# Transformer layer on one core: routing arithmetic spread over three feed-forward units, the first unit's high terms first, one transposed row of maxima earlier

## The reference, cut to what matters

```
xn = _layernorm(x)
a  = sliding_window_attn(xn)                     # 16 heads of 16, window of 64 to each side
h  = layer_norm(a + xn, g1, b1)
f  = gelu(h @ W1 + c1) @ W2 + c2                 # 256 -> 1024 -> 256
attn_out = layer_norm(f + h, g2, b2)
scores = einsum('bsh,eh->bse', xn, gate_w)       # 8 experts, each token goes to one
chosen = argmax(scores)
ffn_out = xn + (xn @ expert_w[chosen].T)         # written as einsum with a one-hot
out = x + attn_out + ffn_out
```

## Time and profile before

| | before |
|---|---|
| median of 3 runs (lowest, highest) | 1375.54 us (1372.25, 1376.72) |
| profiled execution: time, span | 1372.64 us, 1370.9 us |
| mean granted clock of TensorE | 0.968 |
| busy: PE, DVE, ACT, POOL | 1160.1, 899.2, 737.7, 672.8 us |
| share of the chain that ended last: PE, ACT, DVE, issue, POOL, DMA | 55%, 12%, 9%, 7%, 4%, 4% |
| HBM traffic | 122 GB/s over the span |

### The profile page before, as it was taken

How to read it: one execution, slowest core, us unless ns; L and a number is a source line. 1 busy time by engine, 2 the same in 40 slices (tenths; PEclk the granted TensorE clock), 3 DMA queues, 4 the chain that set the end, 5 groups by cost and what they waited for, 6 DMA issues and landing times.

```text
span 1370.9 us, 32155 instructions
## 1 busy us (share of the span) xinstructions
PE 1160.1 (85%) x11726; PEld 704.4 (51%) x11726; DVE 899.2 (66%) x2097; ACT 737.7 (54%) x1498; POOL 672.8 (49%) x864
## 2 busy tenths in 40 slices
PE   0636898899979898798979999899988999799987
PEld 0323446574637546384546646374464746365356
DVE  8563657675677766676577756676576756676355
ACT  1322675448553575537654485627754375645761
POOL 6311565427751465517653375605655277524861
PEclk9956999999999999999999999999999999999999
DMA  8494279234952359234863249433692349513010
GB/s 268 122 214 151 92 142 206 67 109 121 222 140 87 131 110 212 74 117 118 188 166 99 88 118 218 115 109 110 146 198 68 112 122 221 141 54 103 7 28 32
DMA packets 126230, 176.43 MB, mean 129 GB/s; under 512 B 11104, under 2 KB 95968, under 8 KB 122976
## 3 DMA queue, kind: packets, MB, share of 16 engines
q1 hardware_dynamic: 103168, 132.43, 33.4%
q0 software_dynamic: 22912, 41.95, 16.5%
HBM read 82.85 MB, written 85.07 MB: 122 GB/s over the span
## 4 chain that ended last, share of the span: by engine, by line
PE 55%; ACT 12%; DVE 9%; issue 7%; POOL 4%; DMA 4%; another core or an unknown queue 2%; SPq 0%; POOLq 0%; DVEq 0%; ACTq 0%
PE bank L1264 7%; PE bank L1358 7%; PE bank L1164 5%; PE bank L1167 5%; PE bank L1165 5%; ACT pool L1046 5%; PE bank L1438 3%; PE bank L1257 3%; PE bank L1434 3%; PE bank L1435 3%; DVE m_sb L757 2%; PE bank L1232 2%; ACT bank L1101 2%; PE bank L1196 2%
## 5 line engine op out<-in xcount | busy, mean ns | idle before, releaser
L1046 ACT ACTIVATE pool<-bank 128x512 f32<-128x512 f32 x512 | 287.9, 599 | 114.5 <-PE bank L1264 111.6
L757 DVE TENSOR_REDUCE m_sb<-bank 128x2 f32<-128x384 f32 x512 | 260.7, 552 | 98.4 <-PE bank L1272 84.3
L494 POOL TENSOR_SCALAR_AFFINE_SELECT pool<-pool 128x512 f32<-128x512 f32 x256 | 181.7, 710 | 161.8 <-ACT pool L1046 122.4
L432 POOL TENSOR_TENSOR rs<-ve,neghalf 128x1 f32<-128x1 f32 x64 | 36.8, 575 | 324.5 <-DVE ve L834 272.3
L1264 PE MATMUL bank<-q_s,k_s 128*128 128x256 f16 x1024 | 180.6, 276 | 11.1 <-ACT pool L1046 5.3
L1358 PE MATMUL bank<-pool,v_a 128*32 128x256 f32 (+2 forms) x2560 | 159.1, 339 | 11.9 <-POOL pool L499 8.2
L1257 PE MATMUL bank<-k_s,q_s 48*64 48x192 f16 x2048 | 95.5, 262 | 68.9 <-DVE m_sb L757 49.2
L1032 ACT ACTIVATE xn<-bank 128x256 f32<-128x256 f32 x120 | 46.1, 384 | 191.0 <-PE bank L1167 180.9
L1264 PEld LDWEIGHTS bank<-q_s,k_s 128*128 128x128 f16 x1024 | 74.7, 97 | 133.9 <-issue 103.7
L849 DVE TENSOR_TENSOR pool<-bank,pool 128x512 f16<-128x512 f32 x128 | 88.2, 689 | 73.1 <-ACT pool L1060 60.9
L499 POOL TENSOR_SCALAR_AFFINE_SELECT pool<-pool 128x512 f32<-128x512 f32 x208 | 135.3, 650 | 0.0
(11 more groups left out here) (168 smaller groups left out, 2433.2 us busy)
## 6 DMA issues: line engine op xcount, KB each, us to landing
pair_dram<-pool SPq DMA_DIRECT2D x96, 256.0 KB
xn<-xs_dram SPq DMA_DIRECT2D x40, 384.0 KB, 3.7
ys_dram<-xn SPq DMA_DIRECT2D x120, 128.0 KB, 1.8
q_s<-pair_dram SPq DMA_DIRECT2D x32, 384.0 KB
k_s<-pair_dram SPq DMA_DIRECT2D x32, 384.0 KB
x_sb<-in_L_attn_x SPq DMA_DIRECT2D x8, 1024.0 KB, 6.5
res_dram<-in_L_attn_x SPq DMA_DIRECT2D x8, 1024.0 KB, 7.0
res_dram<-xn POOLq DMA_DIRECT2D x8, 1024.0 KB, 8.0
```

What stands on the lines that cost most here:

```text
L494: nc.gpsimd.affine_select(out=p, in_=p, compare_op=ALU.is_ge, fill=0.0, base=0, pattern=[[0, 4], [1, 2 * W]], channel_multiplier=-1).then_ ...
L757: nc.vector.tensor_reduce(m_sb[:, 4 * g + par:4 * g + 4:2, t], max_bank(j, par)[:, 0:2 * WIN].rearrange("p (h c) -> p h c", h=2), AX.X, AL ...
L1046: nc.scalar.activation(prob[:, (k + 2) % 3, par::2, :], TB[par][:, :].rearrange("p (h q) -> p h q", h=2), ACT.Exp, scale=EXP_SCALE).then_i ...
```

## The change

Three things are moved; no arithmetic is added or left out.

1. On DVE, the three pieces of routing no longer stand together ahead of `gelu_low(1)`: tiles come behind `gelu_low(1)`, positions behind `gelu_low(2)`, experts behind `gelu_low(3)`.
2. On PE, unit 0 of W1 waits for the high half alone, runs its four matmuls on `tr_h`, then waits for `tr_l` and runs the other two. (With it, the first projection unit of the next batch waits for three instead of four low halves.)
3. On PE and DVE, `max_cols` of group 2 goes to the head of step 10's new work: ahead of `scores(b, 27)` and of `maxima(b, 27)`.

```diff
@@ vector, d_stage
                         for i in range(2, 4):
                             n1_low(b, i)
-                        if not last:
-                            routing_tiles(b + 1)
-                            routing_positions(b + 1)
                     if u == 1 and not last:
+                        routing_tiles(b + 1)
+                    if u == 2 and not last:
+                        routing_positions(b + 1)
+                    if u == 3 and not last:
                         routing_experts(b + 1)
@@ vector, turn
+                    if k in MAX_AT:
+                        max_cols(b, MAX_AT[k])
                     if 1 <= k and k - 1 + LEAD < STEPS:
                         maxima(b, k - 1 + LEAD)
-                    if k in MAX_AT:
-                        max_cols(b, MAX_AT[k])
@@ tensor, qk_third
-                        pe.wait_ge(xT_l.sem, xT_l.at(b, 4))
+                        pe.wait_ge(xT_l.sem, xT_l.at(b, 3 + u))
@@ tensor, w1_unit
-                pe.wait_ge(nT_l.sem, nT_l.at(b, DC * hf + DC))
                 if u == 0:
+                    pe.wait_ge(nT_h.sem, nT_h.at(b, DC))
                     pe.wait_ge(r1.sem, r1.at(b, T))
+                else:
+                    pe.wait_ge(nT_l.sem, nT_l.at(b, DC * hf + DC))
...
+                if u == 0:
+                    for c in range(DC):
+                        nc.tensor.matmul(UB[0][:, :], w1_h[:, c, fs], tr_h[:, c, s], start=c == 0, stop=False)
+                    for c in range(DC):
+                        nc.tensor.matmul(UB[0][:, :], w1_l[:, c, fs], tr_h[:, c, s], start=False, stop=False)
+                    pe.wait_ge(nT_l.sem, nT_l.at(b, DC))
+                    for c in range(DC):
+                        mm = nc.tensor.matmul(UB[0][:, :], w1_h[:, c, fs], tr_l[:, c, s], start=False, stop=c == DC - 1)
+                    mm.then_inc(u_ps.sem, 1)
+                    return
```

## The result

| | before | after |
|---|---|---|
| median (lowest, highest) | 1374.11 us (1372.25, 1376.72) | 1352.49 us (1350.63, 1353.46) |
| profiled execution: time, span | 1372.64, 1370.9 us | 1350.63, 1348.9 us |
| mean granted clock | 0.968 | 0.968 |

To find where, I cut both traces at marks that every batch has: the start of DVE's one-hot, and PE's four transposes of maxima (groups 0 to 3, `max_cols`).

The account below looks back on a forecast made before the run. The chain is mostly PE, with routing stages set by when POOL's send ends. Terms -5.2 (routing stages) and -2 (step 10) sum to -7.2 on 1372.64, giving 1365.4; median forecast 1368.5 us, range 1354 to 1381.

Parts of the forecast that it names:

- The low-half wait of the projection: Next batch's first projection unit on PE: the wait is hidden behind step 18, gain 0, bounds -0.5 and 0.
- The feed-forward stage: Seven routing stages: unit 8 held instead of unit 7, net 0.75 us earlier each, -5.2 in all.
- a lump for the clock: Routing stage, PE: half clock after its longer stand costs up to 1.7 us, taken as 0.75 per stage.
- The new wait: PE in the routing stage: about 2.4 us for `maxima(2)` ahead of `scores(3)`, none ahead of unit 4.
- Which result is held: Routing stage: `scores(4)` and unit 7 escape the hold; unit 8 and `scores(5)` are held.
- the bound of 6 us: PE results ending from about 6 us behind the first scatter on are seen late by ACT and DVE.
- The release one step sooner: Routing stage: the first held result, unit 8, is released one scatter ahead of the last, 1.4 us earlier.
- The escape: Rival, 13%: unit 8 gets through the hold, some 2.5 us per stage gained, total 1356.
- send later, same results held: Rival, 17%: `scores(4)` or unit 7 held until the later release, unit 10 0.93 us later per stage, 1381.4.
- the moves do not matter: Rival, 10%: PE's new stand ahead of `scores(3)` drops the clock, unit 7 slips, gains and losses cancel, 1375.5.
- Step 10: Moved `max_cols`: PE resumes 1.4 us earlier, counting only in three half-clocked batches of eight, -2 us in all.
- The DMA rule: POOL's scatters: descriptors cannot be written during DVE two-port operations; release 0.2 later instead of 0.93, rows bearing it out half.

Follow-up runs that it names:

- e1: Kernel before with the projection edit alone (units 0 and 1 wait for three and four low halves): 1361.35 us, ratio 0.993 to before.
- e3: Changed kernel with the old routing order on DVE (spread undone): 1356.15 us, ratio 0.990 to the kernel before.
- e6: Kernel before with the routing spread on DVE alone: 1374.19 us, ratio 0.998 to the kernel before.
- e9: Changed kernel with the positions behind `maxima(2)` instead of ahead of it: 1357.25 us, ratio 0.986 to the kernel before.
- e11: Changed kernel with four scatters, then h's eight multiplications, then four scatters in the in-stage sends: 1333.77 us, ratio 0.970 to the kernel before.
- e12: Changed kernel in which POOL waits ahead of the fifth scatter of each send until the first four land: 1334.67 us, ratio 0.973 to before.
- e8: Changed kernel with one of h's eight multiplications behind each scatter of the seven in-stage sends: 1323.41 us, ratio 0.963 to the kernel before.
- e7: Changed kernel with each indirect scatter made a plain transfer to fixed rows, tokens not sorted: 1324.51 us, ratio 0.962 to the kernel before.
- e4: Changed kernel with `max_cols` of group 2 again behind `scores(27)` and `maxima(27)`: 1355.55 us, ratio 0.988 to the kernel before.
- e5: Changed kernel with unit 0 again waiting for the low halves ahead of all its matmuls: 1362.48 us, ratio 0.990 to the kernel before.
- e10: As e8, multiplications between transfers, but with plain transfers to fixed rows in place of the scatters: 1335.68 us (one run).

## Why the prediction was wrong, point by point

- **The failed step** is the sentence "The low-half wait of the projection is hidden, as it stands behind step 18: 0, bounds -0.5 and 0." It is worth 1.17 us in the typical batch (four of the seven stretches, 0.65 to 2.26 in the others), 9.6 in the traces, and 10 in e1's time. The row was there to be read: the waits of before had 8 of them, 8.5 us. I took "behind step 18" for cover. PE's list is in order, though, so the question was not whether the projection is urgent but what stands behind it, and that was the second half of step 18's scores, with ACT idle for them. With 9.6 more, and the 3.1 of the start that comes with the same edit (e1: 3.0), the sum of 1365.4 is 1352.7, beside the profiled 1350.6. The rest, -2.1, is the sum of -1.0 in the feed-forward stages, -2.4 from group 0 to 2, where no run looked for a cause, +0.4 in step 10 and +0.9 at the end.
- **The feed-forward stage** was forecast at -5.2 in all and came at -6.2, a typical stage at -0.75 as forecast. That match is luck: the forecast had it from unit 8 being held in place of unit 7, less a lump for the clock, and neither came so. By e3, unit 0 gives 0.57 of it (forecast 0.45 for DVE's work) and the spread 0.18. The price of a later send was about right: the first scatter is 1.07 later in e6 (forecast 0.94), and in e9, whose send is 0.92 later than the changed kernel's, the stage is 0.95 longer.
- **The new wait** was right: 2.06 us ahead of `scores(3)` (forecast 2.4), none ahead of unit 4. The first scatter starts 231.81 - 220.84 = 10.97 behind unit 0's first matmul, where I said 11.4.
- **Which result is held** was wrong in all seven stages: still unit 7's first. Two things failed. In six of them PE ran at half clock behind its new stand (0.50 for 3.21 us in the first), so that unit 7 ended not 5.2 but 6.8 behind the first scatter (238.04 + 0.59 = 238.63); I had counted the half clock as a lump of 0.75 at the end and not as a delay that puts a unit back into the hold. In the second stage unit 7 did end 5.2 behind, and there the bound of 6 us failed: it was held for 1.86 us (rows below). The bound is the deeper fault, since in e6 unit 7 ended 5.2 behind in six stages, at full clock, and was held for 3.4 to 4.8 us. So without the half clock the forecast's first held result would have been wrong too. The release one step sooner came as said: in the first stage at 241.75, 0.89 behind the last scatter's start instead of 2.39; in the second stage it came at 393.07, ahead of the last scatter.

Second routing stage of the changed kernel, first and last scatter on POOL, unit 7 on PE and its gelu on ACT:

```profile
385.98 1.07 POOL L532 DMA_INDIRECT xs_dram<-xn,pos  x1 [4.92 <-DVE pos L732]
...
390.62 0.59 PE L1168 MATMUL bank<-tr_h,w_l 128*128 128x512 f16 x2
...
393.07 0.66 ACT L1102 ACTIVATE bank<-bank,c1c 128x512 f32<-128x512 f32 x1 [2.32 <-PE bank L1168]
...
395.03 0.97 POOL L532 DMA_INDIRECT xs_dram<-xn,pos  x1 [0.30 <-issue]
```

- **The rivals.** The escape (13%) is real as a mechanism, worth 3.1 to 4.7 us a stage (e11 and e12, e8, e7), but this change does not bring it about; spacing the scatters does. The two rivals in which unit 7 stays held were right on that: "send later, same results held" (17%) in that the start of the hold does not go by time alone, "the moves do not matter" (10%) in that the clock fell behind PE's new stand and unit 7 slipped. Neither had the time (1381.4 and 1375.5): the stage gained, and both left the projection at nothing too. By the sign that the prediction set for the former, unit 10 later than 23.2 from unit 0, its case was just missed: 243.91 - 220.84 = 23.07.
- **Step 10** was right as far as the one stretch shows (e4's time does not tell): PE resumes earlier (its wait is 0.65, not the 0.2 of the forecast, since `maxima(27)` now ends last), ACT's exponential starts 1.00 behind the normalised tile before and after, and the three half-clocked batches gain 0.80 to 0.90 each, 2.6, of which three of the four full-clock ones give back 0.2 each and the last batch 0.5: -1.6 for the forecast's -2.
- **The DMA rule.** The scatter starts 0.86 behind the cast of the positions in both kernels: 235.41 to 236.27 before, with `gelu_low` on DVE in between the earlier trace rows, and 230.95 to 231.81 after, with maxima there. The trace shows the same lag for both, so the agreement that the prediction half saw was chance. The prediction also misapplied the rule. The Trainium skill, "SBUF — State Buffer" (the "DVE blocks DMA" trap), speaks of operations in a two-port mode, and by the same page ("Who interferes with whom") `tensor_tensor` has no such mode. `gelu_low` is a `tensor_tensor`, so by the page neither case is blocked, and the equal lags of 0.86 agree.

## What to carry to other kernels

Price a removed wait by what stands behind it on its in-order engine, and look the wait up in the list of waits by its line, however small the hunk. A wait of 1 us can be worth less or more than its length: the 1.17 ahead of unit 0 was worth 0.57 a stage where the clock stayed full (before and e3) and over 2 where it fell to one half behind the wait (three stages of e5). Where idle time is put down to no engine, vary what another engine issues at that time: spacing eight indirect transfers gave more than the whole change, 29 us beside 22.

## What the hardware showed that was not expected

With eight indirect scatters in a row, 1.28 us apart, PE's results were seen late by ACT and DVE. Those that ended 5.2 or 5.3 us behind the first scatter were late by anything from nothing (unit 6 before) to 4.8 us (unit 7 in e6), those from about 7 on by up to 4.6. The result that was held longest in its stage was seen between 2 us ahead of the last scatter's start (second stage of the changed kernel) and 2.5 behind it (e9). Four and four cost at most 0.5 to 1.0 (e11, e12), and eight spread over 13.5 us nothing (e8). Spacing has a price of its own: beside interleaved multiplications on POOL, three short DVE instructions took 2.25 us in e10 and 1.18 in e8 where they took 0.73 in e7. What fills up, and what picks the result that is held, is open: the fourth scatter of e12 had landed by 3.2 us after its start. Whether a row of five or six would hold, whether plain transfers in as long a row with nothing between them would, and whether the eight gathers of the attention's output, 1.85 us apart, hold anything, was not tried.
